# Routed experts by pairs of full tiles, with the first product in three fp32r passes

## The reference, cut to what matters

```python
H, F, E_SHARED, E_ROUTED, K = (128, 512, 1, 8, 2)
def _expert(x, w_up, w_down):
    h = jax.nn.gelu(jnp.einsum('bsh,hf->bsf', x, w_up), approximate=False)
    return jnp.einsum('bsf,fh->bsh', h, w_down)
probs = jax.nn.softmax(jnp.einsum('bsh,he->bse', x, router_w), axis=-1)
top_k_prob, top_k_idx = jax.lax.top_k(probs, K)
...
for e in range(E_ROUTED):
    y = _expert(x, routed_up[e], routed_down[e])
    routed_out = routed_out + gates[..., e:e + 1] * y
return shared_out + routed_out + x
```

## Time and profile before

| what | value |
|---|---|
| median of 3 runs | 496.35 us |
| profiled execution | 495.9 us, span 493.7 us |
| TensorE busy | 459.5 us (93%) |
| VectorE, ScalarE, GpSimd busy | 309.5, 277.9, 184.8 us |
| slot stage, from the first turn to the last product | 304.6 to 463.2 us |
| mean TensorE clock granted | 0.977 of full |

### The profile page before, as it was taken

The page is one execution under the profiler, slowest core; times in us unless marked ns, Lnnn a source line. Parts: engine busy times, 40 slices in busy tenths (PEclk is TensorE's granted clock), DMA queues, the critical chain, the costliest instruction groups (busy, mean ns, idle before and its releaser), DMA issues.

```text
span 493.7 us, 15314 instructions
## 1 busy us (share of the span) xinstructions
PE 459.5 (93%) x5214; PEld 389.1 (79%) x5215; DVE 309.5 (63%) x1002; ACT 277.9 (56%) x624; POOL 184.8 (37%) x209
## 2 busy tenths in 40 slices
PE   8999999999998999989889999788899999999984
PEld 7688888887786777766579999777799999999631
DVE  5578888888885678888665672333344544455246
ACT  5687867786666989887678542112122332222226
POOL 5512011117000111156656464565545555555300
PEclk9999999999998999999979999898899999999999
DMA  5343136500000161111112123121222222222186
GB/s 140 88 120 99 53 97 132 156 1 4 24 5 19 37 222 45 45 50 56 56 56 70 39 70 90 58 63 60 60 67 65 65 65 69 59 70 60 53 288 203
DMA packets 47879, 37.98 MB, mean 77 GB/s; under 512 B 5456, under 2 KB 41184, under 8 KB 47824
## 3 DMA queue, kind: packets, MB, share of 16 engines
q1 hardware_dynamic: 43072, 28.10, 20.8%
q0 software_dynamic: 4320, 8.92, 5.1%
q10 hardware_dynamic: 432, 0.20, 0.1%
HBM read 19.30 MB, written 16.34 MB: 72 GB/s over the span
## 4 chain that ended last, share of the span: by engine, by line
PE 55%; DVE 21%; ACT 9%; issue 7%; DMA 3%; another core or an unknown queue 2%; DVEq 2%; SPq 0%; POOL 0%; ACTq 0%; POOLq 0%
PE bank L1333 12%; PE bank L1323 12%; PE bank L1283 6%; DVE tkr L1445 2%; DVE negmax L1454 2%; DVE prob L1451 2%; PE bank L1007 2%; PE bank L954 2%; DMA wdn<-routed 2%; PE bank L956 2%; PE bank L955 2%; PE bank L997 2%; PE pair L1315 1%; DVE stats L1593 1%
## 5 line engine op out<-in xcount | busy, mean ns | idle before, releaser
L894 ACT ACTIVATE prob<-bank 128x512 f32<-128x512 f32 x71 | 42.2, 597 | 121.3 <-PE bank L1323 106.8
L574 POOL DMA_INDIRECT routed<-zbuf x71 | 73.6, 1036 | 72.1 <-DVE zbuf L1808 40.3
L1323 PE MATMUL bank<-cT,prob 128*128 128x128 f32 x568 | 78.9, 283 | 8.9 <-DVE prob L1802 7.9
L1333 PE MATMUL bank<-wdn,prob 128*128 x568 | 80.6, 287 | 1.7 <-ACT prob L894 1.5
L1323 PEld LDWEIGHTS bank<-cT,prob 128*128 128x128 f32 x568 | 71.2, 197 | 12.2 <-DVE prob L1802 9.9
L1333 PEld LDWEIGHTS bank<-wdn,prob 128*128 128x128 f32 x568 | 71.4, 197 | 2.9 <-issue 2.2
L1802 DVE COPY prob<-wup 128x512 f32 x71 | 30.6, 430 | 44.6 <-issue 25.4
L1808 DVE TENSOR_SCALAR zbuf<-bank,zbuf 128x128 f32<-128x128 f32 x71 | 24.9, 350 | 46.0 <-PE bank L1333 29.6
L471 POOL DMA_INDIRECT slots<-zbuf,slot x32 | 31.4, 981 | 20.8 <-PE bank L1283 7.6
L471 POOL DMA_INDIRECT slots<-tkr,slot x32 | 31.5, 986 | 13.9 <-issue 6.4
L461 POOL TENSOR_TENSOR hlw<-hst,lnw 128x512 f32<-128x512 f32 x8 | 10.2, 1275 | 63.2 <-ACT hst L784 63.2
(11 more groups left out here) (281 smaller groups left out, 995.0 us busy)
## 6 DMA issues: line engine op xcount, KB each, us to landing
slots<-x2T SPq DMA_DIRECT2D x8, 585.0 KB, 5.3
zbuf<-slots SPq DMA_DIRECT2D x71, 65.0 KB
tkr<-in_x SPq DMA_DIRECT2D x8, 256.0 KB, 2.9
cs<-in_ctx SPq DMA_DIRECT2D x8, 256.0 KB, 2.8
wup<-in_L_ffn_routed_up SPq DMA_DIRECT2D x1, 2048.0 KB, 8.7
zbuf<-tkr SPq DMA_DIRECT2D x8, 256.0 KB
wup<-routed SPq DMA_DIRECT2D x8, 256.0 KB, 3.6
wdn<-routed SPq DMA_DIRECT2D x8, 256.0 KB, 4.0
```

Source lines behind the costliest of these rows:

```text
L574: pool.indirect_dma_start(routed, bass.IndirectOffsetOnAxis(ap=xr[n][:, :].bitcast(I32)[:, DEST:DEST + 1], axis=0), yr[n % 4][:, :], None) ...
L894: act.activation(hT[:, n % 2, :], bank[2 + n % 2][:, :], ACT.Gelu).then_inc(s["hT_ok"], 1)
L1323: m = mm(bank[2 + n % 2][:, c * P:(c + 1) * P], wst[:, n % 2, c * P:(c + 1) * P], xrT[:, n % 2, :], start=True, stop=True)
L1333: m = mm(bank[6 + n % 2][:, 0:D], hT[:, n % 2, c * P:(c + 1) * P], wdn[:, bass.ds(e * (FC * D) + c * D, D)], start=(c == 0), stop=(c == FC ...
```

## The change

The first 50 of the 71 tiles are worked as 25 pairs (`MATES`); a pair is 256 full rows of one expert. The other 21 (`ALONE`) go one by one as before, written out without a loop.

- **Up product.** For a pair, one matmul has 256 moving columns, and its operands are fp32r: high and low parts of the weights (ScalarE `w_high`, VectorE `w_low`) and of the rows (ScalarE `rows_high`, VectorE `rows_low`). Four chunks by three passes make 12 matmuls for two tiles, in the place of 16 matmul instructions. The down product is unchanged: 16 for two tiles.
- **Order.** On TensorE a step is `up_pair(p - 1)`, `turn_pair(p)`, `down_pair(p - 2)`. On ScalarE it is the two Gelus of pair p - 1, then `rows_high(p)`, then `w_high(p + 1)`. On VectorE it is `rows_low(p)`, first `y_out`, `w_low(p + 1)`, second `y_out`.
- **Buffers and loads.** 16 row buffers instead of 8, loaded by one DMA for a pair.
- **Tables.** Four tables in the place of two: pairs 0 to 7 from the first half of the tokens, 8 to 15 from three quarters, 16 to 24 from all, and the 21 single tiles.
- **Scatters.** The eleven left over stand one for each pair of tiles, in the first 22 tiles.
- **Loops.** Pairs 8 to 23 run in a loop of eight pairs (two iterations) on TensorE, VectorE and ScalarE. The rest is written out.

The core of the diff:

```diff
-EARLY = 24
+PAIRS = (8, 16, 25)
+MATES = PAIRS[-1]
+ALONE = SLOT_TILES - 2 * MATES
...
         for t in range(2 * NX):
             rows_out(t, t % NX)
-            if t % 3 < 2 and IN_LOOP + t - t // 3 < 2 * NT:
-                scatter(IN_LOOP + t - t // 3)
+            if t % 2 == 0 and IN_LOOP + t // 2 < 2 * NT:
+                scatter(IN_LOOP + t // 2)
...
-        with act.Fori(0, SLOT_TILES // 2) as i:
-            for n in range(2):
-                gelu(2 * i + n, n)
+        def w_high(p, q):
+            e = act.value_load(texpi[0:1, bass.ds(p, 1)], min_val=0, max_val=E - 1)
+            if not (isinstance(p, int) and p < 2):
+                act.wait_ge(s["up_ps"], 2 * p - 2)
+            act.activation(wst_hi[q], wup[:, bass.ds(e * FF, FF)], ACT.Copy).then_inc(s["wq_ok"], 1)
+        def rows_high(p, q):
+            act.wait_ge(s["xr_ps"], 2 * p + 2)
+            act.activation(xp_hi[q], bank[q][:, 0:2 * P], ACT.Copy).then_inc(s["xhi_ok"], 1)
+        def gelu_pair(p, q):
+            for b in range(2):
+                act.wait_ge(s["up_ps"], 2 * p + b + 1)
+                act.activation(prob[:, 2 * q + b, :], bank[2 + b][:, :], ACT.Gelu).then_inc(s["hT_ok"], 1)
+        def pair_step(p, q, more=True):
+            first = isinstance(p, int) and p == 0
+            if not first:
+                gelu_pair(p - 1, 1 - q)
+            rows_high(p, q)
+            if more and not first:
+                w_high(p + 1, 1 - q)
...
+        def up_pair(p, q):
+            pe.wait_ge(s["wst_ok"], 2 * p + 2)
+            pe.wait_ge(s["xrT_ok"], 2 * p + 2)
+            for c in range(FC):
+                b, k = c // 2, slice(c * P, (c + 1) * P)
+                if c % 2 == 0 and not (isinstance(p, int) and p == 0):
+                    pe.wait_ge(s["hT_ok"], 2 * p - 1 + b)
+                u = bank[2 + b][:, (c % 2) * 2 * P:(c % 2 + 1) * 2 * P]
+                mm(u, wst_hi[q][:, k], xp_hi[q], start=True, stop=False)
+                mm(u, wst_lo[q][:, k], xp_hi[q], start=False, stop=False)
+                m = mm(u, wst_hi[q][:, k], xp_lo[q], start=False, stop=True)
...
+        def pair_step(p, m, i):
+            if not (isinstance(p, int) and p < 1):
+                up_pair(p - 1, (m - 1) % 2)
+            if not (isinstance(p, int) and p < 2):
+                turn_pair(p, m, i)
+            if not (isinstance(p, int) and p < 2):
+                down_pair(p - 2, m % 2)
...
+        def w_low(p, q):
+            e = dve.value_load(texpi[0:1, bass.ds(p, 1)], min_val=0, max_val=E - 1)
+            pause(dve, s["wq_ok"], 5 + p, s["passed_dve"])
+            tt(wst_lo[q], wup[:, bass.ds(e * FF, FF)], wst_hi[q], ALU.subtract).then_inc(s["wst_ok"], 2)
+        def rows_low(p, q):
+            dve.wait_ge(s["xhi_ok"], 2 * NG + 2 + p)
+            tt(xp_lo[q], bank[q][:, 0:2 * P], xp_hi[q], ALU.subtract).then_inc(s["xrT_ok"], 2)
+        def pair_step(p, m, i):
+            known = isinstance(p, int)
+            rows_low(p, m % 2)
+            if not known or p >= 2:
+                t, n = 2 * p - 4, 2 * m - 4
+                y_out(t, n, t // 4 if known else 4 * i + n // 4)
+            if not known or p >= 1 and p + 1 < MATES:
+                w_low(p + 1, (m + 1) % 2)
...
+            if not known or p >= 2:
+                y_out(t + 1, n + 1, (t + 1) // 4 if known else 4 * i + (n + 1) // 4)
```

285 lines of the change are left out of this document (180 added, 105 removed).

## The result

The changed kernel took 486.69 us (median of 4 runs, 484.19 to 489.08), the kernel before 496.73 us beside it (4 runs, 493.66 to 497.13). The ratio on record is 0.984, with a 95% interval of 0.980 to 0.989: 1.6% faster. The four runs of the changed kernel were two near 484 and two at 489, so its middle is uncertain: the two medians as given stand at 0.980. The time lies in the range of the prediction, but the gain is less than the 3.3% that was forecast, at 1.6% less than half of it. The profiled run of the changed kernel took 484.19 us, the fastest of the four, with a span of 482.5.

The account below looks back on a forecast made before the run. TensorE, busy 93% of the span, was taken as the bound. Terms -10.5 - 4.0 - 3.9 + 0.7 + 1.0 = -16.7 from 495.9 gave 479.2, 479.7 as median, stated as 480 us; range 469 to 491.

Parts of the forecast that it names:

- part 1: Up matmuls on TensorE: fewer, 256 columns wide at 0.115 us each, a pair 3.38 us against 3.80; gain 10.5 us.
- part 4: First 24 tiles, scatters among result writes: loss of 14.4 us falls to 10.5, bounds 5.4 and 17.6; gain 3.9 us.
- part 3: Loops behind tile 24: of 5.6 us loop cost 1.6 remain, as fewer iterations run; gain 4.0 us.
- part 5: Tables and start: tables mostly fit idle time, first pair 0.7 us late; change to single tiles costs 1.0 us.
- Part 2: ScalarE (2.8 of 3.38 us a pair) and VectorE (2.4) keep up; rows' chain covered by 0.1 us; nothing charged.
- the first rival: Rows' chain isn't covered on TensorE; 0.3 us wait a pair gives 487 us, 495 with first-stretch losses; chance 15%.
- GpSimd's pace: First 11 pairs: 33 indirect DMAs at 1.26 us take 41.6 us against 37.2, 4.4 us slower; lower bound 5.4 with filling.
- 1 us of filling: Start of the first 24 tiles: filling the pipeline costs about 1 us, counted in the lower bound of 5.4.

Follow-up runs that it names:

- five scatters a group: Changed kernel with five scatters, not four, in six shared-expert groups, five left among the stores; 460.16 us (0.968), in a later set 489.27 us (0.985).
- the second profile of before: The kernel before, unchanged, profiled again in the third set of runs on chip 13; 496.2 us (one run).
- the kernel with six extra transfers: Changed kernel plus six indirect transfers of input rows that nobody waits for, two behind each store of tiles 36, 40 and 44; 465.15 us (one run).

## Why the prediction fell short

The sum was made against the profiled execution of before: -16.7 us. Between the two first profiles the spans differ by 493.7 - 482.5 = 11.2, with the fastest of the four runs of the changed kernel. Point by point:

| step | predicted | measured | from |
|---|---|---|---|
| pairs (part 1) | -10.5 | -9.0 | 25 x (3.80 - 3.44) |
| first 24 tiles (part 4) | -3.9 | -1.5 | loss 14.4, then 54.2 - 41.3 = 12.9 |
| behind them: loops (part 3), change to single tiles (part 5) | -4.0 + 1.0 | +0.6 | extra 5.8 (93.2 - 46 x 1.90), then 89.1 - 13 x 3.44 - 20 x 1.90 = 6.4 |
| start (part 5) | +0.7 | -1.0 | first turn at 303.61, was 304.64 |
| behind the last turn | 0 | -0.2 | |
| sum | -16.7 | -11.1 | |

**Part 1** was right in its mechanism: 0.12 us a matmul, and the prices go by columns. The pair came out at 3.44, not 3.38: the first up matmul of a pair takes 0.20 to the next (384.56 to 384.76), so that up is 1.52, not 1.38; down is 1.70, not 1.78.

**Part 2** was right: no wait in the steady state. By its own test, idle time ahead of the up products released by `rows_low`, the first rival would have been taken for true. It isn't: the releaser is the same, but the cause is a late Gelu ahead of `rows_high` in five pairs, not an uncovered chain in each.

**Part 3** was half right. In the pairs' loops nothing is left to see: with five scatters a group, where no Gelu was late, the turns stand 3.44 us apart across both turns of the loop. The change to single tiles costs what was forecast: the 20 steps take 0.95 us more than 20 x 1.90 there. But what part 3 left was filled again, and in this first profile it is the largest miss: with the change, -3.0 us were forecast and +0.6 came. Of the 6.4 us lost behind the 12th pair, 4.3 are in the pairs, most of it in two that are 1.8 us longer because a Gelu came 1.9 and 1.0 us behind the up products (357.76 to 363.06, and 373.95 to 379.20), and 2.1 among the single tiles (about 1.0 of it the change), where results are written tile by tile and ScalarE stands 3.48 us once (until 416.72). The prediction had put all stalls into the first 24 tiles. In the two later profiles of the changed kernel 9.1 and 8.8 us are lost there. The Trainium skill's page Runtime: NRT & Kernel Launch (Instruction fetch mechanics) has straight code fetched ahead and only far branches stalling; the pairs' loop, at 3.44 us across its turns, agrees with it if its branches are near ones, which no run shows. The 0.84 us of the old loop came back in the second profile of before and stays unexplained.

**Part 4 is the step that failed.** It named the mechanism as its upper bound ("stalls come with indirect DMAs": 33 transfers, 17.6 us) and GpSimd's pace as its lower, and took 10.5 between them. The three profiles of the changed kernel where before takes 495 lost 12.9, 15.4 and 17.8 us (54.2, 56.7 and 59.1 less 41.3): the upper bound was nearly right. What is short in part 3 has the same cause, late Gelus that part 4 had not priced behind the 12th pair. With the mean of the three losses, 15.4, and pairs of 3.44 in the sum, part 4 gives back 1 us and no gain. The argument for a smaller loss (fewer table reads and back edges on ScalarE, scatters no denser) rested on nothing that the trace showed. The row that should have decided was the earlier trace rows: both other engines stand and go on together while GpSimd issues back to back, in a stretch where GpSimd was busy only 32.46 of 60.0 us. An engine that is busy half the time is hardly the limit by its pace over the stretch; where no Gelu was late, that pace cost 2.3 us, and behind the 12th pair. Nor was there 1 us of filling to add: without late Gelus the twelve pairs took 39.4 us, less than 41.3.

**Part 5**: the tables fitted into the idle time whole (`base(6)` starts at 300.24, where it was 301.27), and the start came 1.0 us earlier, not 0.7 later.

Where before takes 476, the changed kernel's loss in the first 24 tiles isn't there: the first twelve pairs of the kernel with six extra transfers take 39.4 us. Where the kernel before gains its 19 us isn't shown, as it was not profiled under that condition. The sum without part 4 is -12.8 us; from 476.3 to 476.8 that is a ratio of 0.973, and the versions of the changed kernel gave 0.968 to 0.975 there. That the sum without part 4 fits is luck in part: its gain from the pairs is 1.5 us too large, and its start 1.7 us too late. The changed kernel itself was never timed under that condition, so that this is a bound from its neighbours: its copy with six more transfers took 465.15 against 476.31.

**What stays open.** Why a whole set of runs has the condition, in three of five sets here and in the first runs, and by which path a row of transfers reaches the other engines. Whether other work on the same chip makes the condition is an obvious question, and nothing on record answers it. The trace shows neither a queue nor a semaphore for the path, and the instruction queues move nothing at the late Gelus of the timeline above (316 to 320 us). The Trainium skill, on the page DMA: Bandwidth & Descriptors (SWDGE vs HWDGE vs iDMA), says that a transfer issued by GpSimd has its descriptors written by software into rings in SBUF, while SyncE's and ScalarE's have theirs from hardware. That fits with GpSimd's transfers being the ones that hurt, and explains neither the other engines' standing nor the condition. Whether plain transfers of GpSimd do the same wasn't seen, as that kernel ran where nothing was late.

No version is shown to beat the changed kernel under both conditions; most ran under one only. Five scatters ahead of the first store had the lowest ratio where before takes 495 (0.975), five a group where it takes 476 (0.968).

## What to carry to other kernels

If engines stand together while GpSimd issues indirect transfers back to back, take the loss as going with the transfers that fall into the stretch, not with time or instructions: here the other engines got faster, the loss stayed or grew (14.4 us before, 12.9 to 17.8 after), and the gain was given back. Look for the kernel's own gaps between such transfers (here waits of GpSimd on TensorE's progress) before removing them: they looked idle, and without them the stage took 40 us longer. And run the kernel before in each set, profile it there, and time a small gain in more than one set: the change is worth 1.3% to 1.6% in one condition, and its nearest versions are 2.5% to 3.2% ahead in the other.

## What the runs showed of the hardware

- Where before takes 495, 27 indirect transfers of 128 rows at 1.26 to 1.31 us from start to start left TensorE 7.10 us busy of 20, ScalarE 3.06 and VectorE 4.50, mostly with 1.0 to 2.4 us between single matmuls, and the mean granted clock at 0.70. In the changed kernel, whose rows there are of at most four, TensorE was busy 20.00 of 20. Where before takes 476, rows of ten and twelve transfers in the same stage left no gap in TensorE's stream.
- The kernel before takes 493 to 499 us in some sets of runs and 475 to 478 in others, and chip 7 had one set of each. Within a set the two didn't mix.
- An fp32r matmul of 256 columns takes 0.12 us and one of 512 0.23, beside a weight load of 0.19.
- A fill of one element between two indirect transfers costs GpSimd nothing (0.09 us within the 0.30 between them); one that it waits for brings the pair from 3.44 to 5.06 us.
